# Attention of a perceiver block in chunks of 512 keys instead of 256, with the opening loads and one copy in another order

## What is computed

```
q = layernorm(x) @ Wq                     # 2 x 64 x 1024
k, v = split(context @ Wkv)               # 2 x 1024 keys x 1024 each
k, v = concat((null_key, k)), concat((null_value, v))
q, k = tanh(q), tanh(k)
attn = softmax(einsum('bhid,bhjd->bhij', q, k) * 64 ** -0.5)
x = x + einsum('bhij,bhjd->bhid', attn, v) @ Wout + bout
```

## Time and profile before

| | us |
|---|---|
| median of 3 runs (lowest, highest) | 204.99 (203.99, 205.06) |
| the profiled execution | 204.92 |
| its span | 203.0 |
| PE busy | 192.7 |
| DVE busy | 142.5 |
| ACT busy | 116.2 |

### The profile page before, as it was taken

How to read it: one execution, slowest core, us unless ns; L and a number is a source line. 1 busy time by engine, 2 the same in 40 slices (tenths; PEclk the granted TensorE clock), 3 DMA queues, 4 the chain that set the end, 5 groups by cost and what they waited for, 6 DMA issues and landing times.

```text
span 203.0 us, 4247 instructions
## 1 busy us (share of the span) xinstructions
PE 192.7 (95%) x1667; PEld 147.0 (72%) x1669; DVE 142.5 (70%) x259; ACT 116.2 (57%) x217; POOL 47.4 (23%) x48
## 2 busy tenths in 40 slices
PE   7999889999999999999999999999986999999991
PEld 2698779988998889988998767866753454544680
DVE  2679899989888899999878699435777825404313
ACT  2389999777977798778877672026430133222200
POOL 5636024220222062202202950021321300000001
PEclk9999999999999999999999999999999699999998
DMA  6945984934691110010000799999999400000000
GB/s 207 390 110 128 281 187 118 365 108 124 185 343 35 52 52 3 0 55 0 5 0 2 242 386 264 386 375 377 381 377 378 150 0 3 0 0 0 5 0 26
DMA packets 20836, 30.95 MB, mean 152 GB/s; under 512 B 1841, under 2 KB 15570, under 8 KB 20818
## 3 DMA queue, kind: packets, MB, share of 16 engines
q1 hardware_dynamic: 20098, 29.12, 44.1%
q10 hardware_dynamic: 720, 1.57, 2.1%
HBM read 29.51 MB, written 0.13 MB: 146 GB/s over the span
## 4 chain that ended last, share of the span: by engine, by line
PE 59%; issue 21%; DVE 11%; ACT 4%; POOL 2%; DMA 2%; POOLq 0%; DVEq 0%; ACTq 0%
PE ps L1101 39%; PE ps L1135 6%; PE ps L1200 2%; DVE keys L799 2%; PE ps L1175 2%; PE ps L1191 2%; PE ps L1089 2%; DVE att L949 2%; DMA x<-in_x 2%; DVE ex_sum L822 1%; ACT keys L621 1%; DVE ex_l L765 1%; PE ps L1163 1%; DVE lo L974 1%; PE ps L1312 1%
## 5 line engine op out<-in xcount | busy, mean ns | idle before, releaser
L799 DVE SCALAR_TENSOR_TENSOR keys<-ps,keys 64x512 f16<-64x512 f32 x64 | 44.1, 688 | 2.9 <-ACT keys L621 0.9
L621 ACT ACTIVATE keys<-ps 64x512 f16<-64x512 f32 x64 | 37.9, 593 | 1.8
L1101 PE MATMUL ps<-ctxT_h,w_k_h 128*128 128x256 f32 x128 | 37.9, 296 | 0.0
L1101 PE MATMUL ps<-ctxT_h,w_k_l 128*128 128x256 f32 x128 | 36.2, 282 | 0.0
L1101 PE MATMUL ps<-ctxT_l,w_k_h 128*128 128x256 f32 x128 | 36.1, 282 | 0.0
L765 DVE TENSOR_TENSOR ex_l<-ps,ex_h 128x512 fp32r<-128x512 f32 x32 | 22.0, 688 | 9.7 <-ACT ps L661 9.6
L660 ACT ACTIVATE ex_h<-ps 128x512 fp32r<-128x512 f32 x32 | 19.1, 597 | 13.9 <-PE ps L1135 13.7
L1101 PE MATMUL ps<-ex_h,ctx_h 128*128 128x512 f32 x64 | 25.3, 396 | 0.0
L1101 PE MATMUL ps<-ex_l,ctx_h 128*128 128x512 f32 x64 | 25.1, 392 | 0.0
L1101 PE MATMUL ps<-ex_h,ctx_l 128*128 128x512 f32 x64 | 24.9, 389 | 0.0
L1101 PEld LDWEIGHTS ps<-ctxT_h,w_k_h 128*128 128x128 f32 x128 | 24.4, 191 | 0.2
(11 more groups left out here) (189 smaller groups left out, 272.9 us busy)
## 6 DMA issues: line engine op xcount, KB each, us to landing
w<-in_fc1T SPq DMA_DIRECT2D x8, 1024.0 KB, 12.4
w<-in_fc SPq DMA_DIRECT2D x8, 1024.0 KB, 12.3
stage_n<-in_ctx SPq DMA_DIRECT2D x8, 256.0 KB, 2.9
stage_t<-in_ctxT SPq DMA_DIRECT2D x7, 256.0 KB, 4.4
q_two<-q_split SPq DMA_DIRECT2D x8, 128.0 KB, 2.3
w_v<-in_Wv SPq DMA_DIRECT2D x1, 1024.0 KB, 5.4
w_out<-in_Wout SPq DMA_DIRECT2D x1, 1024.0 KB, 8.1
const<-in_const SPq DMA_DIRECT2D x1, 968.0 KB, 6.6
```

The costliest lines, as they stand in the source:

```text
L621: nc.scalar.activation(keys[rows, u % 2, PK * i:PK * (i + 1), r], full[rows].rearrange("p (j n) -> p j n", j=PK), ACT.Copy, scale=UNIT).th ...
L799: V.scalar_tensor_tensor(out=keys[other, u % 2, PK * i:PK * (i + 1), r], in0=ps[mine, K_BANK + kp % 2].rearrange("p (j n) -> p j n", j=PK) ...
L1101: last = MM(dst, lhs[i], rhs[j], start=start and m == 0, stop=stop and m == len(parts) - 1)
```

## The change

A chunk has CK = 512 keys and a unit KT = 4 steps, so there are 8 units and still 32 steps. `project_keys(kp)` now makes one pair of heads by 512 keys: 6 matmuls of 512 columns instead of 12 of 256. AHEAD becomes 5, and the opening projects five steps before the first scores. The transposed context is loaded, cast and subtracted in pieces of 512 keys (4 instead of 8, each 128 x 1024 elements); the context itself stays in pieces of 256 keys (`CN`, `NN`, `KN`). The key weights stay in four pieces of the same size, each now two steps' worth. The identity is loaded by ACT's queue ahead of the first transposed chunk, and the copy of `xnT` moves from DVE to ACT, behind the split of the first weight piece.

```diff
-CK = 256
+CK = 512
+CN = 256
...
-            sp.dma_start(const[:, 0:C_ONES], a["eye"]).then_inc(ld_eye, 16)
...
+            act.dma_start(const[:, 0:C_ONES], a["eye"]).then_inc(ld_eye, 16)
             act.dma_start(stage_t[:, 0], ctxT_source(0)).then_inc(ld_ctxT[0], 16)
...
             split_wk(0)
+            act.wait_ge(xnT_psum, 1)
+            copy(xnT[:], ps[:, 0, 0:DC * P].rearrange("p (c t) -> p c t", c=DC), xnT_ready)
             split_wk(1)
...
-            dve.wait_ge(xnT_psum, 1)
-            V.tensor_copy(xnT[:], ps[:, 0, 0:DC * P].rearrange("p (c t) -> p c t", c=DC)).then_inc(xnT_ready, 1)
...
             split_queries(1)
-            high_ctxT(1)
             high_ctx(0)
             low_keys(2)
+            high_ctxT(1)
+            for kp in range(3, AHEAD):
+                low_keys(kp)
...
+            next_ctx = {0: 1, 4: 2, 5: 3, 8: 4, 9: 5, 12: 6, 13: 7}
+            next_ctxT = {3: 2, 7: 3}
+            left = {7: 2, 9: 3}
+            for v in range(PAIRS):
+                for s in range(2 * v, 2 * v + 2):
                     low_exponentials(s)
-                for kp in range(KT * u + AHEAD, min(KT * (u + 1) + AHEAD, STEPS)):
+                for kp in range(2 * v + AHEAD, min(2 * v + AHEAD + 2, STEPS)):
                     low_keys(kp)
...
+            for kp in range(2, AHEAD):
+                project_keys(kp)
+            for v in range(PAIRS):
+                scores(2 * v)
+                if v < G:
+                    null_scores(v)
+                scores(2 * v + 1)
+                for kp in range(2 * v + AHEAD, min(2 * v + AHEAD + 2, STEPS)):
                     project_keys(kp)
...
+                if v >= 1:
+                    pe.wait_ge(null_ready, min(v, G))
+                    for s in range(2 * v - 2, 2 * v):
+                        weighted_sum(s)
```

More of the change, by code:

```diff
@@ L50 @@
 PK = PG // KT
+PIECES = 4
 LH, LDK, LDV, LR = 4, 64, 128, 16
@@ L246, in block_kernel @@
         ld_wq = [sem(f"ld_wq{half}") for half in range(2)]
-        ld_wk = [sem(f"ld_wk{i}") for i in range(G * KT)]
-        ld_ctx = [sem(f"ld_ctx{n}") for n in range(B * NC)]
+        ld_wk = [sem(f"ld_wk{i}") for i in range(PIECES)]
+        ld_ctx = [sem(f"ld_ctx{n}") for n in range(B * NN)]
         ld_ctxT = [sem(f"ld_ctxT{n}") for n in range(B * NC)]
@@ L276, in block_kernel @@
         wk_later = sem("wk_later")
-        wk_ready = [sem(f"wk_ready{i}") for i in range(G * KT)]
+        wk_ready = [sem(f"wk_ready{i}") for i in range(PIECES)]
         ctxT_high = sem("ctxT_high")
@@ L472, in _ @@
             sp.dma_start(w_route[:], chunked("wg")).then_inc(ld_lin, 16)
-            for n in range(5, B * NC):
-                if n + 1 < B * NC:
-                    load_ctxT(n + 1)
+            for n in range(4, B * NN):
                 load_ctx(n)
@@ L651, in _ @@
             queries_tanh(1)
-            keys_tanh(2)
+            for kp in range(2, AHEAD):
+                keys_tanh(kp)
             def exponentials(s):
@@ L661, in exponentials @@
                 nc.scalar.activation(full, full, ACT.Exp, scale=SCORE_SCALE).then_inc(e_ready, 1)
-            for s in range(SINGLES):
-                exponentials(s)
-                if s < G:
-                    null_exp(s)
-                keys_tanh(s + AHEAD)
-            for u in range(SINGLES // KT, NU):
-                for s in range(KT * u, KT * (u + 1)):
-                    exponentials(s)
-                for kp in range(KT * u + AHEAD, min(KT * (u + 1) + AHEAD, STEPS)):
+            for v in range(PAIRS):
+                exponentials(2 * v)
+                if v < G:
+                    null_exp(v)
+                exponentials(2 * v + 1)
+                for kp in range(2 * v + AHEAD, min(2 * v + AHEAD + 2, STEPS)):
                     keys_tanh(kp)
@@ L855, in low_exponentials @@
                 add_to_sum(s)
-            def convert_context(u):
-                b, c, g = units[u]
-                n = b * NC + c
-                if g == 0 and n + 2 < B * NC:
-                    high_ctxT(n + 2)
-                if g == G - 1 and n + 1 < B * NC:
-                    high_ctx(n + 1)
-            for s in range(SINGLES):
-                low_exponentials(s)
-                low_keys(s + AHEAD)
-                if s % KT == KT - 1:
-                    convert_context(s // KT)
-            for u in range(SINGLES // KT, NU):
-                for s in range(KT * u, KT * (u + 1)):
+            next_ctx = {0: 1, 4: 2, 5: 3, 8: 4, 9: 5, 12: 6, 13: 7}
[3 more added lines that the diff above has]
+                for s in range(2 * v, 2 * v + 2):
                     low_exponentials(s)
-                for kp in range(KT * u + AHEAD, min(KT * (u + 1) + AHEAD, STEPS)):
+                for kp in range(2 * v + AHEAD, min(2 * v + AHEAD + 2, STEPS)):
                     low_keys(kp)
-                convert_context(u)
-                if units[u - 2][1] == NC - 1:
-                    evacuate(u - 2)
+                if v in next_ctxT:
+                    high_ctxT(next_ctxT[v])
+                if v in next_ctx:
+                    high_ctx(next_ctx[v])
+                if v in left:
+                    evacuate(left[v])
             dve.wait_ge(ld_small, 16 * (5 + E))
@@ L1111, in project_keys @@
                     pe.wait_ge(ctxT_ready, n)
-                pe.wait_ge(wk_ready[KT * g + i], 1)
+                piece, half = 2 * g + i // 2, i % 2
+                pe.wait_ge(wk_ready[piece], 1)
                 if kp >= 2:
@@ L1115, in project_keys @@
                 for j in range(PK):
-                    cols = slice(j * P, (j + 1) * P)
+                    cols = slice(half * P, (half + 1) * P)
                     for d in range(DC):
                         last = split_product(ps[:, K_BANK + kp % 2, j * CK:(j + 1) * CK],
-                                             [w[:, KT * g + i, d, cols] for w in (w_k_h, w_k_l)],
+                                             [w[:, piece, d, cols] for w in (w_k_h, w_k_l)],
                                              [x[:, n % 2, d, :] for x in (ctxT_h, ctxT_l)], d == 0, d == DC - 1)
@@ L1150, in weighted_sum @@
                     cols = slice(half * P, (half + 1) * P)
-                    last = split_product(ps[:, mix_bank(half, g)], [x[:, n % 2, t, cols] for x in (ctx_h, ctx_l)],
+                    last = split_product(ps[:, mix_bank(half, g)], [x[:, n % 2, t % KN, cols] for x in (ctx_h, ctx_l)],
                                          [x[:, s % NE, :] for x in (ex_h, ex_l)], c == 0 and t == 0,
```

96 lines of the change are left out of this document (42 added, 54 removed).

## The result

| | before | after |
|---|---|---|
| median of 20 runs each, side by side (us) | 204.90 | 206.26 |
| the profiled execution (us) | 204.92 | 206.42 |
| its span (us) | 203.0 | 204.4 |
| start of the values' projection in it (us) | 124.29 | 125.65 |

The account below looks back on a forecast made before the run. PE was taken to bound the pairs, ACT and DVE the opening. Opening +1.25 net, pairs -1.37, last pairs +0.8 and stall +0.07 gave +0.8 us on a 204.99 median: 205.8 us, range 203.8 to 207.2.

Parts of the forecast that it names:

- the net term of the opening: Opening until PE leads: scores of step 6 come 4.2 us later, but two fewer projections (2.96 us) remain: +1.25 us net.
- The term of the last pairs: Pair 14: its first weighted sum waits for POOL's subtraction of the last context piece, +0.8 us, bounds 0.3 and 1.1.
- The pairs: PE-led pairs: 12 matmuls of 512 columns shorten each from 6.65 to 6.52 us, -1.37 us over 21 projections.
- DVE in pairs with the wide cast: Pairs 3 and 7: the wide cast of `ctxT_h` costs nothing, up to 1.0 us if the cover is gone.
- The opening, until the first projection: Loads, then ACT and DVE: chunk lands at 5.5, weights at 7.0, queries start 8.1, projection 9.9: +0.1 us.
- The rival of a late opening: Opening: first weights at 8 or chunk at 6.5 move everything there by 1 us, to 206.8; chance 0.22.
- a chain that runs over loads in the opening: Opening: a sign named in advance that would show the prediction wrong; no size given.
- its bound of -0.7 for weights at 6.2: Opening until the first projection: if the first weights land at 6.2, it gains 0.7 us instead of losing 0.1.
- The opening, until PE leads: Steps 0 to 7: ACT idles 0.95 us before step 4's tanh at 20.8; scores of step 6 start at 40.6.
- The stall before pair 14: Wait for the last keys before pair 14 grows by 0.07 us, since the projection is shorter.
- The sum: Whole kernel: 1.25 - 1.37 + 0.8 + 0.07 = +0.8 us, to 205.8 us against the median.

Follow-up runs that it names:

- the last pair of experiments: Changed kernel with xn normalised and copied first and last context casts early, 1.0064; the same with DVE's low keys of step 2 before the context cast, 1.0011.
- the last three experiments: Kernel before with only the xnT copy on ACT, 0.9944; changed kernel with xn first and casts early, 1.0064; the latter with step 2's low keys first, 1.0011.

## Why the prediction was right in direction and short in size

The large terms of the sum had their sign and their place; what failed was the size of the loss. The step that failed is the net term of the opening, +1.25, which measured +1.65, and in it the estimate of when the first loads land. The term of the last pairs was short as well, +0.8 for +1.04.

- **The pairs: right.** Forecast 6.52 us and -1.37 in all; measured 6.51, and 6.65 again with narrow matmuls. By the Trainium skill, TensorE: Matmul & The Clock Gate, section Back-to-back issue gap, N/2.4 + 2.5 ns a matmul, a pair would gain an estimated 24 ns; this trace has 135.
- **DVE in pairs with the wide cast: right at nothing.** No wait of PE for DVE between 41 and 106 us; ten pairs average 6.513.
- **The opening, until the first projection: the step that failed.** I had +0.1 for it, from "the chunk ... estimated 5.5" and "the weights ... estimated 7.0". They landed at 6.18 and 7.35; queries and projection came at 8.30 and 10.11, +0.3. I had added up kilobytes in ACT's queue alone. The experiments show that this isn't how it goes: the identity at its head, 64 KB, moved the weights by 3 us in one kernel (4.97 to 8.04), in the changed kernel they came 1.8 us later than with the old loads and the 512 KB of query weights on SP's queue 1.5 us earlier (6.4 for 7.9), and with 512 KB at the head of ACT's queue x landed 1.7 us later in SP's. The rival of a late opening named weights later than 7.2 as the point from which it decides, and this is where they were, at 0.3 of its 1 us. The prediction had also named a chain that runs over loads in the opening as a sign of being wrong; the chain of the changed kernel begins with 5.68 us of one. And its bound of -0.7 for weights at 6.2 doesn't follow from its own walk: with the chunk at 5.5 the transposes end at 7.3, so the queries could start 0.3 us earlier than before at most.
- **The opening, until PE leads: right in mechanism, 0.3 us short.** ACT's idle time before step 4 was 1.11 for 0.95, its tanh at 21.11 for 20.8, the scores of step 6 at 40.99 for 40.6. Of the 0.39 us, 0.2 come from the first projection; the rest are handovers of 0.1 us that a walk by durations leaves out. The net term of the opening, +1.25, measured 4.61 - 2.96 = +1.65.
- **The last pairs: right in place, cause and engine, 0.24 short.** Keys done 5.75 us after the scores of pair 13, cast and subtraction over at 7.51 (forecast 7.5). PE's matmul started 0.15 us behind that, so the wait was 0.94 and not 0.8; and the 12 matmuls behind it took 2.85 us instead of 2.75, the first after an idle stretch being slower to its successor (0.31). Moving the casts took 0.8 us back in the profile.
- **The stall before pair 14**, +0.07 forecast: pair 13 took 5.77 against 5.78, so nothing.

The sum was +0.82, the profiles show +1.36: +0.40 in the opening, +0.24 in pair 14, -0.1 in the rest. The runs show +1.4 and +1.9, each with 0.5 to either side. The larger figure is 0.5 us more than the profile has. Both profiled executions of the changed kernel are among its quick ones: without the fall of the clock (last section) the first would be at 205.3 us, where the thirteen executions without it took 204.98 to 207.08, with a median of 205.94. What lengthens the others is left open.

## What to carry to other kernels

Wider matmuls pay per instruction and not per column, and such a gain is easy to read from two starts in a timeline; but larger units lengthen everything that has to happen before the first and after the last of them, and here that cost about twice the gain, 2.7 us against 1.37. In an opening, put nothing that only needs small, early data behind something that waits for a large load, on any engine: the copy of `xnT` moved for the better and the load order moved with it for the worse, and only taking the two apart showed a version faster than both kernels. When a load order changes, write down in what order all queues together issue, and price the landing by a range of a microsecond or more. And before an experiment's profile is taken for its effect, see where the profiled execution lies among the others.

## What the hardware showed unexpectedly

**The granted clock falls in some executions, behind the linear attention, and costs 1.1 us.** The two kernels of the last pair of experiments run the same program behind the values. Windows of both, the first kernel above, the second below (busy PE, PEld, DVE, ACT, POOL, granted clock, DMA share, GB/s):

```profile
154.00:156.00 2.00, 0.53 (x4) 0.37 (x4) 1.26 (x6) 0.06 (x1) 0.56 (x1) 1.00 1.03 407
156.00:158.00 2.00, 1.86 (x12) 1.02 (x11) 1.14 (x6) 0.46 (x3) 0.00 (x0) 1.00 1.06 354
158.00:160.00 2.00, 1.87 (x13) 0.94 (x10) 1.79 (x10) 0.17 (x2) 0.00 (x0) 1.00 0.70 218
```

```profile
154.00:156.00 2.00, 0.81 (x4) 0.36 (x4) 1.29 (x5) 0.34 (x1) 0.56 (x1) 1.00 1.01 396
156.00:158.00 2.00, 1.96 (x11) 1.21 (x11) 0.86 (x6) 0.35 (x3) 0.00 (x0) 0.70 1.09 358
158.00:160.00 2.00, 2.00 (x6) 0.66 (x5) 1.82 (x10) 0.00 (x0) 0.00 (x0) 0.50 0.48 153
```

In both PE is mostly idle around 155 us, waiting for `xn`. In the second the clock then stands at 0.50, its level of 1.2 GHz, for some 3 us, and returns to 2.4 GHz by 162. From the values to the end it takes 202.5 - 123.74 = 78.8 us, in the first 201.7 - 124.02 = 77.7. All eleven other profiled executions are one or the other: 78.7 to 78.8 us (before, changed, and three more) or 77.7 us (the rest). The changed kernel itself was both: 204.4 - 125.65 = 78.8 in its first profile, 203.3 - 125.63 = 77.7 in the second. So a difference of 1 us between two spans can be this and nothing else; the start of the values told the kernels apart where the spans didn't. The mean granted clock of a whole execution tells which it was: 0.987 to 0.989 in the six profiled ones with the fall, 0.993 to 1.000 in the seven without. Beside the last three experiments 14 of 29 executions of before had 0.989 or less, of the kernel with the new copy alone 1 of 12. The others took 203.81 us on average before and 203.03 with the new copy: 0.78 us less, as the start of the values has it. So of its 0.56% some 0.4% are the copy, and the rest is that the clock fell less often in it.

**DVE slows beside POOL.** The subtraction of `ctxT_l`, 128x512, took 1.76 us in the earlier trace rows, where POOL's subtraction of the weights had begun 0.18 us ahead of it, at 5.68. With the new copy alone POOL began at 6.18, 0.35 us behind DVE, and DVE's took 0.68. `xn` took 1.34 us instead of 0.41 beside the same operation of POOL, which had begun 0.06 us ahead. It goes the other way too: in the kernel with the weights on SP's queue DVE's wide subtraction began at 6.09 and took 1.23 us, and POOL's, begun at 6.27, took 2.17 instead of 1.27. In these four it was the one that began second that slowed.

**A small load that changes queues can delay a large one by far more than its size.** 64 KB moved from SP's queue to the head of ACT's, ahead of 256 KB of context, moved the first cast from 4.67 to 5.95 us and the first split of the weights behind it from 4.97 to 8.04; with the old loads again it was 5.48. The 64 KB alone don't explain it; the 512 KB on the other queue that got in front are the likely reason, as told above. x, the first load on SP's queue, depends on the first one on ACT's in the same way: its statistics started at 3.18 to 3.36 us beside 64 KB there, at 3.88 and 3.92 beside 256 KB, at 4.96 beside 512 KB.
